# Graph network on one Trainium2 core: the last gathers read rows of three bfloat16 parts, and the inward pass gathers by step

## The reference

```python
def _srgnn_conv(x, W, b, src, dst, num_nodes):
    xl = x @ W.T + b
    msgs = xl[src]
    agg = jax.ops.segment_sum(msgs, dst, num_segments=num_nodes)
    cnt = jax.ops.segment_sum(jnp.ones((src.shape[0],), x.dtype), dst, num_segments=num_nodes)
    return agg / jnp.maximum(cnt, 1.0)[:, None]
...
input_in = _srgnn_conv(hidden, W_in, b_in, src, dst, n)
input_out = _srgnn_conv(hidden, W_out, b_out, dst, src, n)
```

## Time and profile before

| | us |
|---|---|
| median of 3 runs | 7637.69 |
| lowest, highest | 7620.69, 7654.07 |
| span of the profiled execution | 7527.2 |
| first gather of `last_gathers` to the end of its last sum (4803.5 to 7327.2) | 2523.7 |

### The profile page before, as it was taken

One profiled execution on the slowest core, in us unless ns is written; L12 is line 12 of the kernel. 1 busy time (PEld: TensorE's weight loads), 2 busy tenths in 40 slices (PEclk: granted clock), 3 DMA queues, 4 the chain that ended last, 5 costly groups with the idle time before them and its releaser, 6 DMA issues. The chain is left out here.

```text
span 7527.2 us, 81611 instructions
## 1 busy us (share of the span) xinstructions
PE 5373.7 (71%) x17807; PEld 3065.0 (41%) x17807; DVE 3160.7 (42%) x6956; ACT 545.2 (7%) x1542; POOL 4732.4 (63%) x4778
## 2 busy tenths in 40 slices
PE   5666777638765556636566687788888888888887
PEld 2333333525332223324444575433433344444444
DVE  2222444528655556674444567511111123333317
ACT  0000000324000000010000001100000000000004
POOL 5666665664666666677677404766666666666665
PEclk8777777969767777767778899865555588888869
DMA  4444433331688888846667675433333333333445
GB/s 137 133 134 130 124 123 121 128 100 66 214 256 256 265 262 268 266 134 210 210 217 226 205 191 148 126 89 89 90 89 87 89 111 119 119 119 119 123 101 191
DMA packets 693161, 1164.20 MB, mean 155 GB/s; under 512 B 104128, under 2 KB 490285, under 8 KB 692614
## 3 DMA queue, kind: packets, MB, share of 16 engines
q0 software_dynamic: 224288, 633.55, 28.9%
q1 hardware_dynamic: 468344, 525.21, 21.9%
q10 hardware_dynamic: 110, 0.23, 0.0%
HBM read 870.83 MB, written 287.77 MB: 154 GB/s over the span
## 5 line engine op out<-in xcount | busy, mean ns | idle before, releaser
L2126 PE MATMUL l_sums<-big 128*128 (+1 forms) x3520 | 1701.9, 578 | 349.1 <-issue 135.1
L195 DVE TENSOR_TENSOR big<-iota_row,dst_tab 128x512 f32<-128x512 f32 x660 | 458.4, 695 | 2171.3 <-PE l_sums L2126 712.1
L1280 POOL DMA_INDIRECT bin_rows<-staging,place_tab x832 | 979.6, 1177 | 337.4 <-issue 249.1
L1166 POOL DMA_INDIRECT big<-kv_rows,idx_tab x880 | 832.0, 945 | 503.0 <-issue 241.1
L578 POOL DMA_INDIRECT big<-in_x,big x832 | 826.6, 994 | 483.6 <-SPq L148 237.7
L2083 POOL DMA_INDIRECT big<-x_rows,place_tab x880 | 882.3, 1003 | 394.9 <-issue 241.7
L2083 POOL DMA_INDIRECT big<-x_rows,idx_tab x832 | 817.2, 982 | 426.7 <-issue 226.6
L1220 PE MATMUL es_q<-big 128*128 x1760 | 720.9, 536 | 450.3 <-issue 343.3
L2126 PEld LDWEIGHTS l_sums<-big 128*128 128x128 f32 x3520 | 765.2, 259 | 502.0 <-issue 473.7
L612 PE MATMUL l_sums<-big 128*128 x1760 | 723.0, 543 | 331.9 <-issue 235.8
L1504 PE MATMUL ws_sums<-big 128*128 128x264 f32 x1760 | 546.1, 474 | 321.2 <-DVE big L1524 170.9
(11 more groups left out here) (297 smaller groups left out, 5187.4 us busy)
## 6 DMA issues: line engine op xcount, KB each, us to landing
v_edge<-big SPq DMA_DIRECT2D x880, 128.0 KB
big<-v_edge SPq DMA_DIRECT2D x220, 512.0 KB
bin_rows<-big SPq DMA_DIRECT2D x110, 520.0 KB
sims<-bin_rows SPq DMA_DIRECT2D x110, 520.0 KB
staging<-in_edges SPq DMA_DIRECT2D x104, 520.0 KB
gate_rows<-big SPq DMA_DIRECT2D x49, 512.0 KB
big<-gate_rows SPq DMA_DIRECT2D x49, 512.0 KB
big<-kv_rows,idx_tab POOLq DMA_INDIRECT x880
```

Source lines behind the costliest of these rows:

```text
L195: return dve.tensor_tensor(out, rows, columns.unsqueeze(2).to_broadcast([P, QUAD, P]), ALU.is_equal)
L1166: pool.indirect_dma_start(ring[:, u, :], None, k.kv_rows, bass.IndirectOffsetOnAxis(ap=k.idx[:, s:s + 1], axis=0)).then_inc(s_row[u], 16)
L1280: pool.indirect_dma_start(k.bin_rows, bass.IndirectOffsetOnAxis(ap=k.place[:, c:c + 1], axis=0), k.staging[:, g % 2, j, :], None).then_inc ...
L2126: pe.matmul(sums[:, bank_of(node[u] + turn, D)], onehot[:, u % HALF, :], flat[:, bass.ds(at, D)], start=False, stop=True, skip_group_check ...
```

## The change

`attend_close` also writes the new state as three bfloat16 parts. The first (ACT, `high_part`, lag 5) is the state rounded to bfloat16; DVE subtracts it (`take_high`, lag 6); ACT rounds the rest (`middle_part`, lag 6); DVE subtracts that and rounds what is left (`low_part`, lag 7). SP writes the three parts as one row of 1.5 KB for each node to a new tensor `x3_parts` (`send_parts`, lag 8), beside the float32 rows, which `last_gathers` and `gru_close` go on reading for the gates.

In `last_gathers` both passes gather rows of `x3_parts`. DVE's matrices of zeros and ones are written as bfloat16, and each step has three bfloat16 products of 256 columns in place of one float32 product; only the third adds to `s_sum`. The inward pass has one gather for each step (880 in place of 832), through `k.idx`, which keeps the index by step that `edge_scores` used, as `attr_sums` no longer overwrites it. POOL waits on `s_sum` and PE on `s_row[u]` in both passes; SP's relays, `last_row` and `push` are gone.

```diff
@@ attend_close, SP
-            over(sp, (load, 0), (send, 6))
+            def send_parts(w, slot, nodes):
+                sp.wait_ge(s_low, w + 1)
+                sp.dma_start(k.x3_parts[bass.ds(w * P, P), :], parts[:, slot, :]).then_inc(s_parts[slot], 16)
+
+            over(sp, (load, 0), (send, 6), (send_parts, 8))
             sp.wait_ge(s_sent, 16 * NW)
+            for slot in range(S):
+                sp.wait_ge(s_parts[slot], 16 * len(range(slot, NW, S)))
@@ attend_close, ACT
-            over(act, (second_root, 3), (first_root, 2), (copy_turned, 0))
+            def high_part(w, slot, nodes):
+
+                act.wait_ge(s_new, w + 1)
+                if not early(w, S):
+                    act.wait_ge(s_parts[slot], turns(w, slot, 1))
+                act.copy(parts[:, slot, 0:D], x[:, node_window(w)]).then_inc(s_high, 1)
+
+            def middle_part(w, slot, nodes):
+
+                act.wait_ge(s_rest, w + 1)
+                act.copy(parts[:, slot, D:2 * D], rest[:, slot, :]).then_inc(s_middle, 1)
+
+            over(act, (second_root, 3), (first_root, 2), (copy_turned, 0), (high_part, 5), (middle_part, 6))
@@ attend_close, DVE
+            def take_high(w, slot, nodes):
+
+                dve.wait_ge(s_high, w + 1)
+                dve.tensor_tensor(rest[:, slot, :], x[:, node_window(w)], parts[:, slot, 0:D],
+                                  ALU.subtract).then_inc(s_rest, 1)
+
+            def low_part(w, slot, nodes):
+
+                dve.wait_ge(s_middle, w + 1)
+                dve.tensor_tensor(parts[:, slot, 2 * D:], rest[:, slot, :], parts[:, slot, D:2 * D],
+                                  ALU.subtract).then_inc(s_low, 1)
+
...
-                 (second_moments, 3))
+                 (second_moments, 3), (take_high, 6), (low_part, 7))
@@ last_gathers, POOL
-            for n in range(NC + STEPS):
-                u = n % U
-                column = k.idx[:, n:n + 1] if n < NC else k.idx2[:, n - NC:n - NC + 1]
-                if u % QUAD == 0 and n >= U:
-
-                    if n < NC + U:
-                        pool.wait_ge(s_used, n + QUAD - U)
-                    else:
-                        pool.wait_ge(s_sum, STEPS + (n - NC) + QUAD - U + 1)
-                pool.indirect_dma_start(ring[:, u, :], None, k.x3_rows, bass.IndirectOffsetOnAxis(
+            for t in range(2 * STEPS):
+                u = t % U
+                column = k.idx[:, t:t + 1] if t < STEPS else k.idx2[:, t - STEPS:t - STEPS + 1]
+                if u % QUAD == 0 and t >= U:
+
+                    pool.wait_ge(s_sum, t + QUAD - U + 1)
+                pool.indirect_dma_start(ring[:, u, :], None, k.x3_parts, bass.IndirectOffsetOnAxis(
                     ap=column, axis=0)).then_inc(s_row[u], 16)
@@ last_gathers, SP
-            sp.sem_inc(s_here, HERE)
-            sp.wait_ge(s_lasts, 16)
-            lasts = None
-            for c in range(NC):
-                lasts = relay_chunk(nc, sp, lasts, lasts_row, c, s_row, row0, s_here, s_sum, s_used)
-            for c in range(NC - BEHIND, NC):
-                lasts = relay_used(nc, sp, lasts, lasts_row, c, s_sum, s_used)
             work.sync(sp)
@@ last_gathers, PE
-                if turn:
-                    pe.wait_ge(s_row[u], row0 + NC + 16 * ((t - STEPS) // U + 1))
-                else:
-                    chunk_ready(pe, t, node[u], s_here)
-                at = u * D if turn else slot_of(t, node[u], D)
+                pe.wait_ge(s_row[u], row0 + 16 * (t // U + 1))
+                at = u * PARTS * D
                 if t % QUAD == 0:
                     pe.wait_ge(s_hot, t + QUAD)
                 pe.wait_ge(s_free, (node[u] & NODE_BITS) + turn * NW)
-                pe.matmul(sums[:, bank_of(node[u] + turn, D)], onehot[:, u % HALF, :], flat[:, bass.ds(at, D)],
-                          start=False, stop=True, skip_group_check=True).then_inc(s_sum, 1)
-                push(pe, k, spare[:, 0:1])
+                for n in range(PARTS):
+                    ins = pe.matmul(sums[:, bank_of(node[u] + turn, D)], onehot[:, u % HALF, :], flat[:, bass.ds(at + n * D, D)],
+                                    start=False, stop=True, skip_group_check=True)
+                ins.then_inc(s_sum, 1)
```

More of the change, by code:

```diff
@@ L55 @@
 DEGMAX = 511
+PARTS = 3
 assert (NW - 1 - 4) % 4 == 0
@@ L172, in clear_banks @@
     pe.sem_inc(s_sum, 1)
-def push(pe, k, spare):
-    ones = k.ones.bitcast(BF16)
-    pe.matmul(spare, ones[:, 0:1], ones[:, 0:1], start=True, stop=True)
 def take_banks(act, k, ends, sums, width, place, s_sum, s_taken, s_free, turn=0):
@@ L1543, in attr_sums @@
         sums = psum(nc, ctx, "as_sums", [P, BANKS * BANK])
-        s_zeros, s_one, s_src, s_rel, s_hot, s_sum, s_taken, s_free, s_sources = sems(
-            nc, k, *(f"as_{n}" for n in ("zeros", "one", "src", "rel", "hot", "sum", "taken", "free", "sources")))
+        s_zeros, s_one, s_src, s_rel, s_hot, s_sum, s_taken, s_free = sems(
+            nc, k, *(f"as_{n}" for n in ("zeros", "one", "src", "rel", "hot", "sum", "taken", "free")))
         s_in = sems(nc, k, *(f"as_in{n}" for n in range(RING)))
@@ L1634, in attend_close @@
         part = sets.take([P, S, D])
+        parts = sets.take([P, S, PARTS * D], BF16)
+        rest = room.take([P, S, D])
         tps = [psum(nc, ctx, f"ac_t{i}", [P, 512]) for i in range(2)]
@@ L1647, in attend_close @@
         s_gate = sems(nc, k, *(f"nt_gate{i}" for i in range(S)))
+        s_high, s_rest, s_middle, s_low = sems(nc, k, *(f"sp_{n}" for n in ("high", "rest", "middle", "low")))
+        s_parts = sems(nc, k, *(f"sp_sent{i}" for i in range(S)))
         block = ctx.enter_context(nc.Block())
@@ L2054, in last_gathers @@
         room = Arena(k.side)
-        ring = room.take([P, U, D])
+        ring = room.take([P, U, PARTS * D], BF16)
         flat = ring.rearrange("p u d -> p (u d)")
-        onehot = room.take([P, HALF, P])
-        lasts_row = room.take([1, NC], I32)
+        onehot = room.take([P, HALF, P], BF16)
         zeros = room.take([1, BANK])
         sums = psum(nc, ctx, "l3_sums", [P, BANKS * BANK])
-        spare = psum(nc, ctx, "l3_spare", [1, BANK])
-        s_zeros, s_hot, s_sum, s_taken, s_free, s_lasts, s_here, s_used = sems(nc, k, *(f"l3_{n}" for n in (
-            "zeros", "hot", "sum", "taken", "free", "lasts", "here", "used")))
+        s_zeros, s_hot, s_sum, s_taken, s_free = sems(nc, k, *(f"l3_{n}" for n in (
+            "zeros", "hot", "sum", "taken", "free")))
         s_row, row0 = k.s_row, k.rows_before
-        k.rows_before += NC + 16 * IT
+        k.rows_before += 32 * IT
         k.gate = gate_weights(k)
```

9 lines of the change are left out of this document (2 added, 7 removed).

## The result

The changed kernel takes 7666.25 us (median of 13 runs) against 7628.23 us (median of 13 runs measured beside it): a ratio of 1.0052, 95% interval 1.0034 to 1.0070. The prediction was 7517 us; the change costs some 38 us where 121 were to be won. The measured time lies inside the stated range of 7400 to 7700 us, but only because that range took in the rivals.

What follows compares the result with a forecast made beforehand. The prediction took both passes to be bound by PE, with stalls and POOL close behind. Its terms, `attend_close` +39, inward pass -94 and outward pass -66, sum to -121 us: 7637.7 to 7517 us, range 7400 to 7700.

Steps and rivals of the forecast that it cites:

- What bounds the kernel: Both `last_gathers` passes: bound by PE (1.25 us a step inward), with stalls it can't make up, POOL close behind.
- The account of the outward pass: Outward pass before the change: PE's gates, steps and stalls at clock 0.86 give 23.1 us a row, measured 23.5.
- The ring, up to 12 gathers or 15 us, now hides stalls of 2 to 6 us: Inward pass: with PE faster, POOL becomes the bound and its gathers ahead cover the stalls; inward sum 1140 against 1233.9 us.
- 5 us left over inward and 40 outward: Time still charged for PE after the change: 5 us inward; outward 0.8 us for each of 49 rows.
- the stalls are not PE's to make up: Rival, both passes: stalls hold POOL 2.5 us a row as now, passes keep their time; +60, 7698 us; chance 8%.
- The 48 gathers: Inward pass: gathers added by going step by step, 48 x 1.25 = 60 us of POOL.
- PE's step: Both passes: three bfloat16 products take 0.90 us at the lower clock, 0.55 at the higher.
- `attend_close`, +39 (0 to 69): Two more DVE subtractions a window at 0.38 us each, 37 us, plus 2 us at the end.
- The outward pass, -66: Outward pass: POOL 1150 us, plus 40 for PE and 34 at the end, 1224 against 1289.8.
- The 34 us for late landings at the end: End of outward pass: some 24 gathers land slowly, 2.66 us each, after POOL's last issue (bounds 13 and 34).
- Dearer rows (third rival): Gathers of 1.5 KB rows cost more to issue; at half as much again +832 us, 8349; chance 5%.
- The lower clock outward (first rival): PE falls to the lower clock in the outward pass, deciding below a mean of 0.66; +240, 7878 us; chance 7%.

Runs made afterwards that it cites:

- e5: The kernel before, unchanged, run again for its trace: 6655 us.
- e14: The changed kernel with four settings in turn per pass (as changed, PE additions of 4, 16 matrices, POOL 8 ahead): 7675 us beside 7593.
- e8: The kernel before with the three parts and three bfloat16 products, inward gathers still by chunk through SP's relays: 7784 us beside 7622, ratio 1.0197.
- e7: The kernel before with the change's `attend_close`, its parts read by nobody: 6689 us, ratio 1.0045.
- e16: Same kernel as e15, run again: 7624 us beside 7519.
- e15: The changed kernel with four settings by rows (as changed, POOL memset per gather, POOL wait every 16th gather, inward SP additions): 6817 us beside 6656.
- e1: The changed kernel with PE adding 4 to `s_sum` at every fourth step instead of 1 each step: 6734 us, ratio 1.0117.
- e4: The kernel before with float32 rows gathered by step, without relays or push; no parts, one float32 product a step: 6699 us, ratio 1.0066.
- e6: The changed kernel, unchanged, run again: 6726 us, ratio 1.0111.
- e17: The changed kernel with three unread bfloat16 products before PE's own work per window in `attend_close`: 6734 us, ratio 1.0101.

## Why the prediction was wrong

**What bounds the kernel: wrong.** "Both passes are bound by PE, with stalls that it can't make up, and POOL is close behind." Without late counts POOL gathers every 1.27 us inward in the kernel before and never stops (e5): POOL was the bound. With late counts both kernels gather inward every 1.44 to 1.48 us, and POOL's loss did not react to the matrices or to the ring (e14). Nor did it react to PE's pace in the outward pass, where both kernels gather alike: PE was busy for 1084 us before and 745 after, and POOL's stops came to 150 us before (the 84 of the earlier trace rows and 67 more that the view calls "remote", which the prediction left out) and 161 after. The line for the 67:

```profile
POOL big L2083 <- remote: 66.7, 27, 3.6
```

PE's 1.25 us a step, the same as POOL's in the earlier trace rows, was a coincidence: the inward clock was at its lower level, where PE just keeps up. (The account of the outward pass also took 0.86 for its clock, which is that of the window up to 7190; over the whole pass it was 0.82.)

**"The ring, up to 12 gathers or 15 us, now hides stalls of 2 to 6 us": the step that failed.** This assumed that a stall has a length of its own. In the sum the stalls stand as 5 us left over inward and 40 outward. Measured were 141 us of stops in 44 waits inward and 153 in 63 outward, behind counts up to 14 us late: POOL ran on until its ring was full by the old count, and then stopped for up to 4.4 us all the same. Why the counts are late stays open. The rival "the stalls are not PE's to make up" is what happened: it gave 7698 at 8%, and the measured time lies between it and the kernel before. Its price of 2.5 us a row (16 x 0.16) is near e14's 16 x (1.44 - 1.25) = 3.0. The reason given against it did not hold: that POOL stands still only when its ring is full. That is true of each stop and says nothing of their sum.

**The 48 gathers: right in size, hidden in the wrong sum.** 60 us were charged and then drowned in a gain of 154 from PE. Measured +52 without late counts. With late counts 48 x 1.44 = 69, less the fall from 1.48 to 1.44 for each of the 832 others (38), leaves 31. That only divides the measured +31; that the 38 are the relays' is likely after e8 but not measured by itself.

**PE's step: the sizes were too high, without effect.** 0.90 and 0.55 us were taken for three products; twelve products, four steps, take 2.74 us at the lower clock, 0.64 a step from start to start, and 1.60 at the higher, 0.37 a step.

**`attend_close`, +39 (0 to 69): right in size, in part by luck.** +38 in the trace of after, +32 in e7 by the time, +9 in the shortest trace. The mechanism was in the bounds and not in the value: each subtraction costs 0.41 or 0.85 us by what POOL does beside it, and 0.38 each is near the mean only because L1782 and L1790 give something back.

**The outward pass, -66:** +3; with POOL the bound nothing could come of PE. The 34 us for late landings at the end were too many: from the end of POOL's last issue to the last sum it was 12 us before and 10 after (16 in e6). **Dearer rows (third rival):** no; 982 and 1003 ns before, 987 and 998 after. **The lower clock outward (first rival):** over the whole pass the clock fell from 0.82 to 0.75, above the 0.66 from which it would decide. **Nothing said that the relays might be cheap.** In e5 they wait 2.4 us in all.

## What to carry to other kernels

When two engines show the same pace, look for the one whose pace is the same in every stage: POOL's 1.25 us a gather stood in all of them, PE's changed with its clock. Before a faster engine is credited with hiding stalls, ask what ends one: here the loss stayed the same with faster products, with 16 matrices for 8 and with a ring of 8 gathers for 16, and behind relays faster products made it worse. And an edit that adds operations to the engine that bounds, here 48 gathers and 98 subtractions, must pay for them at once.

## What the runs showed of the hardware

- A semaphore addition by PE can reach DVE and POOL 14 us after its product (5410.1 to 5424.46 in after), while gathers are issued back to back. Then gathers without relays get through at 1.42 to 1.50 us each instead of 1.25 to 1.30, whatever the rings. Whether this happens was not the kernel's doing: beside before at 7519 to 7628 us it did, beside 6655 to 6672 us never. Nor was it the chip's number: chips 4 and 13 showed both (e14 and e15, e16 and e1).
- The loss is 15%: 7628 against 6657 us for one program. The verdict on the change depends on it: ratio 1.0052 with late counts, 1.0111 without. The kernel before is the fastest of all that were run beside it, in both; e4 was not run with late counts.
- A gather of 128 rows takes POOL 0.946 us and 0.305 to the next, whether the rows have 1, 1.5 or 2 KB, and inward a memset of 128x2 (0.12 us) between two fits into the 0.305 (e15).
- A DVE subtraction of 128x256 with both inputs in SBUF takes 0.41 to 0.45 us beside a gather of POOL and 0.85 beside one of its additions (e6, e17).
